# One label tile fetched row by row by the sync engine in place of the last indirect gather

## The reference

```python
inputs = front_emb[movie_id[:, 0]]
labels = target_movie_id[:, 0]
true_w = after_emb[labels]
true_b = after_bias[labels]
samp_w = after_emb[sampled_ids]
samp_b = after_bias[sampled_ids]
true_logits = jnp.sum(inputs * true_w, axis=-1) + true_b
sampled_logits = jnp.einsum('bd,sd->bs', inputs, samp_w) + samp_b
true_logits = true_logits - jnp.log(expected_count(labels))
sampled_logits = sampled_logits - jnp.log(expected_count(sampled_ids))[None, :]
hits = sampled_ids[None, :] == labels[:, None]
sampled_logits = jnp.where(hits, sampled_logits + NEG_INF, sampled_logits)
logits = jnp.concatenate([true_logits[:, None], sampled_logits], axis=1)
loss = jax.nn.logsumexp(logits, axis=1) - logits[:, 0]
```

## Time and profile before

| | |
|---|---|
| three timed runs | 61.21, 61.70, 62.15 us; median 61.7 |
| profiled execution | 60.37 us |
| its span | 58.6 us, 616 instructions |
| busy, share of the span | DVE 80%, ACT 74%, POOL 68%, PE 60% |
| granted TensorE clock | 0.97 of full speed |

### The profile page before, as it was taken

The page is one execution under the profiler, slowest core; times in us unless marked ns, Lnnn a source line. Parts: engine busy times, 40 slices in busy tenths (PEclk is TensorE's granted clock), DMA queues, the critical chain, the costliest instruction groups (busy, mean ns, idle before and its releaser), DMA issues.

```text
span 58.6 us, 616 instructions
## 1 busy us (share of the span) xinstructions
PE 34.9 (60%) x137; PEld 22.6 (39%) x137; DVE 47.1 (80%) x140; ACT 43.2 (74%) x72; POOL 39.6 (68%) x48
## 2 busy tenths in 40 slices
PE   0000184966962679996969786997699949700000
PEld 0000134513610547753747373766375728400000
DVE  3799888899987319999939999999699999990730
ACT  4304999892871039999999799999999995958020
POOL 4076777776777776777777677777776777776000
PEclk9999999999999999999999999999999999999855
DMA  0581111111001110000100000111100111111000
GB/s 0 165 190 40 23 23 37 30 30 23 22 22 32 35 22 22 22 22 22 45 22 22 22 22 23 28 37 34 31 23 23 23 23 46 23 23 23 23 0 6
DMA packets 1715, 1.91 MB, mean 33 GB/s; under 512 B 944, under 2 KB 944, under 8 KB 1712
## 3 DMA queue, kind: packets, MB, share of 16 engines
q0 software_dynamic: 1280, 1.33, 9.5%
q1 hardware_dynamic: 432, 0.55, 3.7%
HBM read 1.87 MB, written 0.01 MB: 32 GB/s over the span
## 4 chain that ended last, share of the span: by engine, by line
ACT 54%; DVE 23%; DMA 7%; PE 7%; issue 4%; SPq 1%; DVEq 0%
ACT psum L329 23%; ACT masks L312 13%; ACT masks L307 11%; DMA sample_ids<-sample_row 7%; DVE wT_low L390 5%; DVE psum L497 5%; ACT xT L325 4%; DVE masks L384 4%; PE psum L276 2%; PE psum L278 2%; PE psum L277 2%; ACT wT_high L319 1%; DVE b_split L398 1%; DVE b_parts L486 1%; DVE b_split L399 1%
## 5 line engine op out<-in xcount | busy, mean ns | idle before, releaser
L497 DVE CUSTOM_DVE_ANT_0 psum<-psum,masks 128x1024 f32<-128x1024 f32 x16 | 19.4, 1226 | 0.1
L218 POOL DMA_INDIRECT t_rows<-after,rows x16 | 15.6, 974 | 4.9 <-issue 4.9
L218 POOL DMA_INDIRECT x_rows<-front,rows x16 | 15.4, 963 | 4.9 <-issue 4.9
L329 ACT ACTIVATE psum<-psum,lowest 128x1024 f32<-128x1024 f32 x16 | 17.2, 1078 | 1.9 <-DVE lowest L497 1.8
L276 PE MATMUL psum<-wT_high,xT 128*128 128x512 f32 x32 | 13.8, 430 | 6.2 <-ACT psum L329 4.1
L278 PE MATMUL psum<-b_parts,ones 128*128 128x512 f32 x32 | 12.7, 396 | 0.0
L277 PE MATMUL psum<-wT_low,xT 128*128 128x512 f32 x32 | 12.6, 394 | 0.0
L307 ACT ACTIVATE masks<-sample_ids,neg_label 128x1024 f32<-128x1024 int32 x8 | 9.2, 1145 | 3.3 <-DMA sample_ids<-sample_row 3.3
L218 POOL DMA_INDIRECT w_rows<-after,rows x8 | 7.7, 967 | 3.8 <-issue 2.1
L276 PEld LDWEIGHTS psum<-wT_high,xT 128*128 128x128 f32 x32 | 6.0, 187 | 10.8 <-issue 7.3
L312 ACT ACTIVATE masks<-masks,ln_big 128x1024 f32<-128x1024 f32 x8 | 9.2, 1150 | 0.1
(11 more groups left out here) (80 smaller groups left out, 34.0 us busy)
## 6 DMA issues: line engine op xcount, KB each, us to landing
sample_ids<-sample_row SPq DMA_DIRECT2D x1, 512.0 KB, 4.1
x_rows<-front,rows POOLq DMA_INDIRECT x16, 2.4
t_rows<-after,rows POOLq DMA_INDIRECT x16, 2.4
w_rows<-after,rows POOLq DMA_INDIRECT x8, 2.4
id_cols<-ids SPq DMA_DIRECT2D x1, 20.0 KB, 1.6
out<-loss SPq DMA_DIRECT2D x1, 8.0 KB, 1.4
```

The source lines that it names most:

```text
L218: return pool.indirect_dma_start(dst, None, table, bass.IndirectOffsetOnAxis(ap=rows[:, col:col + 1], axis=0))
L329: nc.scalar.activation(logits(t), logits(t), ACT.Exp, bias=lowest[:, t:t + 1], scale=-1.0, accum_out=sums[:, t:t + 1]).then_inc(exp_ok, 1)
L497: V.tensor_tensor_reduce(out=logits(t), in0=logits(t), in1=masks[:, t, :], scale=1.0, scalar=3e38, op0=ALU.add, op1=ALU.min, accum_out=low ...
```

## The change

Label tile 15 is no longer gathered by POOL, which issues 39 gathers instead of 40. Its 128 label numbers come in a second time as one line on one partition (`line_ids`, a DMA between the two loads that SP has had). DVE turns the line into row numbers, three instructions behind `neg_label`, with a table of limits that POOL writes in one more `iota`. SP then waits for `line_rows_ok` and, 128 times, loads one row number into a register and issues one DMA of 1 x 65 floats from that row of the table into one partition of `t_rows`. Each of the 128 DMAs adds 16 to `line_t_in`; the last `dot` waits until it is 2048. SP's wait for `loss_ok` and the store stand behind the loop.

```diff
+SP_TILE, SP_GROUP = 15, 6
...
+        line_ids = sb("line_ids", [1, P], i32)
+        line_wrap = sb("line_wrap", [1, P])
+        line_limits = sb("line_limits", [1, P], i32)
+        line_low = sb("line_low", [1, P])
+        line_rows = sb("line_rows", [1, P], i32)
...
             sp.dma_start(id_cols[:, :], ids).then_inc(ids_in, 16)
+            sp.dma_start(line_ids[:, :], line).then_inc(line_in, 16)
             sp.dma_start(sample_ids[:, :], sample_row.rearrange("(a n) -> a n", a=1).to_broadcast([P, SAMPLES])
                          ).then_inc(row_in, 16)
+            sp.wait_ge(line_rows_ok, 1)
+            for p in range(P):
+                row = sp.value_load(line_rows[0:1, p:p + 1], min_val=0, max_val=VOCAB + SPREAD - 1)
+                sp.dma_start(t_rows[p:p + 1, SP_TILE, :], after[bass.ds(row, 1), :]).then_inc(line_t_in, 16)
             sp.wait_ge(loss_ok, 1)
...
+            pool.iota(line_limits[:, :], pattern=[[1, P]], base=VOCAB - 1, channel_multiplier=0).then_inc(line_limits_ok, 1)
...
                 for t in range(a, b):
-                    gather(t_rows[:, t, :], after, LAB + t).then_inc(t_in[k], 16)
+                    if t != SP_TILE:
+                        gather(t_rows[:, t, :], after, LAB + t).then_inc(t_in[k], 16)
...
+            dve.wait_ge(line_in, 16)
+            dve.wait_ge(line_limits_ok, 1)
+            V.tensor_scalar(line_wrap[:, :], line_ids[:, :], 0.0, float(VOCAB), ALU.is_lt, ALU.mult)
+            link(V.scalar_tensor_tensor(line_low[:, :], line_ids[:, :], float(-VOCAB), line_limits[:, :], ALU.max, ALU.min))
+            V.tensor_tensor(line_rows[:, :], line_low[:, :], line_wrap[:, :], ALU.add).then_inc(line_rows_ok, 1)
...
-                dve.wait_ge(t_in[k], 16 * (b - a))
+                if k == SP_GROUP:
+                    dve.wait_ge(line_t_in, 16 * P)
+                else:
+                    dve.wait_ge(t_in[k], 16 * (b - a))
...
+        "line": got["r_target_movie_id"].reshape(P, TILES)[:, SP_TILE].reshape(1, P),
```

More of the change, by code:

```diff
@@ L34, with log_uniform_loss @@
 LN2_LOW, LN2_HIGH = -0.00021219444, 0.6933594
-def log_uniform_loss(nc, ids, sample_row, front, after, out):
+def log_uniform_loss(nc, ids, line, sample_row, front, after, out):
     f32, f32r, i32 = mybir.dt.float32, mybir.dt.float32r, mybir.dt.int32
@@ L154, in log_uniform_loss @@
         row_in = sem("row_in")
+        line_in = sem("line_in")
+        line_rows_ok = sem("line_rows_ok")
+        line_t_in = sem("line_t_in")
+        line_limits_ok = sem("line_limits_ok")
         limits_ok = sem("limits_ok")
```

## The result

The changed kernel takes 171.45 us (median of 4 runs, 171.34 to 172.77) against 61.56 us for the kernel before: 2.81 times as long, 95% interval 2.78 to 2.84. Forecast were 137.7 us and a range of 80 to 195, with 0.96 on slower. The mechanism was right. One row costs SP more than was taken, 1.26 us in place of 1.00. Single executions of one kernel differ by more than 1.5% at times, so in what follows a ratio compares only the quicker ones of both kernels, while medians are over all.

The account below looks back on a forecast made before the run. Bound before by ACT (54% of the span) and DVE (23%); the change adds SP's serial loop: 0.40 issue, 0.45 load, 0.15 register instructions make 1.00 us a row, 128 rows plus 9.7 give 137.7 us, range 80 to 195.

Parts of the forecast that it names:

- 128 c + 9.7 us: Whole kernel's time: 128 rows on SP plus the start, last landing, last dot product and end; 137.7 us.
- c: SP's time for one row of the loop: load, three register instructions, DMA issue; 1.00 us, bounds 0.41 to 1.72.
- DMA issue: SP's issue of each row's DMA in the loop: taken 0.40 us, bounds 0.35 and 0.43.
- Register load: SP's load of each row number from SBUF, not covered by the same row's work: taken 0.45 us, bounds 0 and 1.05.
- Register instructions: Three per row on SP between load and DMA issue: 0.05 us each, 0.15 together, bounds 0.02 to 0.08 each.
- The delay: At the kernel's start, the line's DMA and three DVE instructions move the ACT and DVE branches back about 0.43 us.
- the gain against it: At the kernel's end, the last dot product no longer waits for POOL's last gather: 0.16 us at most.
- Rival 1: SP's loop is hidden, with cheap one-row issues and loads running ahead, c below 0.40: 60.6 us; chance 0.04.
- the 0.40 from which the loop decides: SP's loop sets the kernel's time once c exceeds 0.40 us, where the last row meets the fourth dot product at 55.66.
- Rival 2: In SP's loop the load costs nothing and the issue counts, c = 0.50 us: 73.7 us; chance 0.08.
- Rival 3: In SP's loop each load costs a whole memory trip, c = 1.72 us: 229.9 us; chance 0.08.
- A queue that fills up: Sign of a wrong mechanism in SP's loop: the spacing of the DMA issues grows along the loop; no size given.

Follow-up runs that it names:

- e7: Changed kernel with the start kept, SP's loop removed and POOL making all 40 gathers: 62.11 us, ratio 1.011 to the kernel before.
- e5: Changed kernel without the 128 register loads, each DMA fetching a fixed table row, timed in rounds: 62.61 us, ratio 1.023 to the kernel before.
- e10: Changed kernel without load checks, four loads ahead of their four DMAs: 152.8 us, disturbed up to 58 us; 0.79 us a row from 60 us on.
- e6: Changed kernel with SP fetching only 32 rows and POOL's 40th gather the other 96: 62.45 us, ratio 1.015 to the kernel before.
- e1: Changed kernel without the 128 register loads, each DMA fetching a fixed table row: 97.9 us beside 94.9 us for the kernel before.

## Why the prediction was right

**What bounds, and what the loop does.** Right. SP's queue and its gaps hold 95% of the chain, DVE waits for the last row, and the time follows 128 c + 9.7 us: with the measured c of 1.262 it gives 171.2, against 171.46 for the profiled execution. The working around c held: the loop began at 3.9 instead of 3.6, and the last dot product started 1.3 us after the start of the last issue (165.09 to 166.39) instead of 1.5.

**What one row costs.** This is the term that was mis-sized, 1.00 for 1.26:
- DMA issue: taken 0.40, measured 0.27. "It hardly goes with the bytes, so I don't expect 260 bytes to be much cheaper" failed. The three rows of before all had 128 partitions, and this DMA has one; it also has far fewer bytes than any of them. Since 8 and 512 KB cost nearly the same, the partitions are the likelier reason, but no run separates the two.
- Register load: taken 0.45, measured 0.478. Right by luck: it was taken from the time of a DMA behind its issue, which nothing in the runs ties to a load. A load costs 0.26 to 0.27, and the rest is the surcharge behind a DMA.
- Register instructions: taken 0.15 for three, measured 0.24 for four (0.152, 0.018, 0.042, 0.029). The fused compare of the check alone is 0.152, outside the bounds of 0.02 to 0.08. The move was in no list.
- Gaps: not in the sum at all. Six of 0.04 us are 0.25 us, the largest single error. The 0.02 us of "issue" in the chain of before was taken as the cost of a register instruction; on SP a gap of about 0.04 us stands behind each instruction, beside its duration.

So -0.13 + 0.03 + 0.09 + 0.25 leaves 1.24, and the rows that took longer bring 1.26. The issue was priced too high, and that took back a third of what the other parts missed.

**The start.** The delay was put at 0.43 us and was 0.9 at `base` in e7, 0.8 at the end of its span; the gain against it was put at 0.16 and was 0.12. The three instructions cost 0.65 us in place of 0.45: one partition with 128 numbers takes longer (0.21 to 0.28 us) than 128 partitions with 40 (0.18 to 0.20). In the changed kernel's TENSOR_SCALAR rows 128x24 takes 0.16 us, 128x40 0.18, 1x128 0.21 and 128x1024 0.77: the time grows with the numbers per partition, not with all of them. POOL's gathers were to stay where they were; the last of the 39 began at 52.06 instead of 51.70, which costs nothing here. The delay of ACT's first mask by 0.43 us didn't come: it started at 5.36 instead of 5.27, because `sample_ids` landed 3.7 us after its issue instead of 4.1.

**The rivals.** Rival 1 was better than its 0.04 in one half: e5 shows that 128 issues alone do fit (0.298 us, below the 0.40 from which the loop decides). Its other half, loads that run ahead, is what e10 refutes: they cost their 0.27 us each, one behind the other. Rival 2 (c = 0.50) needed a load for nothing. Rival 3 (c = 1.72) priced a load at 1.05 us; it is about half of that even behind a DMA. A queue that fills up would have made the spacing grow; in the changed kernel it is 1.26 or 1.27 us in each quarter of the loop.

## What to carry to other kernels

An idle engine is not a free one: ask how many instructions it has to execute in the idle time, and count each with the gap behind it. Here there were 51 us for 128 rows, 0.40 us each, and six instructions with their gaps are 1.24. 32 rows were hidden (e6), but what prepares them stood on the path of DVE and cost more (0.8 us in e7) than the gather's end was worth (0.12 us); a part of the gather doesn't even save that, since the 40th gather stays. The loop of loads and dependent DMAs on SP was serial throughout, so what helps is fewer instructions per row (no check: 0.30 us less) and loads that stand together (0.17 us less again), but the indirect gathers on POOL start 1.25 us apart, for 128 rows each.

## What the runs showed of the hardware that was not expected

- By medians, a register load took 0.26 to 0.27 us behind another load or behind register work, 0.48 to 0.53 us directly behind a DMA issue, and 0.43 us as the first load behind a DMA with 3 or 15 fillers between them. The Trainium skill ("DMA: Bandwidth & Descriptors", section "Latency and other measured facts") puts a floor of about 600 ns under a `tensor_load`; the medians here are all below it and only single loads above (0.66 us in the changed kernel, 0.69 in e10), so the trace disagrees, and the measurement decides. The unrolling by four that it names there as a remedy brought 0.17 us a row, not by overlap but by sparing three of four surcharges.
- A DMA issue of one partition took SP 0.22 to 0.27 us by medians (0.31 us for the 1x128 line), of 128 partitions 0.35 to 0.43 us.
- On two chips the kernel before took 95 us, not 61, and in the traces of the kernels run beside it SP's instructions were late until about 58 us, about as long as POOL's gathers are under way. In e1's, DVE, ACT and PE have long waits too, while POOL's gathers start 1.25 us apart as ever. Whether the gathers have to do with it wasn't tried.
